# Sorting tokens by expert on the chip, in a two-layer transformer kernel on one core

## What is computed

```python
def _L0_ffn_ref(x, Wg, bg, We, be):
    probs = jax.nn.softmax(x @ Wg + bg, axis=-1)
    idx = jnp.argmax(probs, axis=-1)
    p = jnp.take_along_axis(probs, idx[..., None], axis=-1)[..., 0]
    e_idx = idx % We.shape[0]
    h = jax.nn.relu(jnp.einsum('bsd,edf->besf', x, We) + be[None, :, None, :])
    onehot = jax.nn.one_hot(e_idx, We.shape[0], dtype=x.dtype)
    out = jnp.einsum('besf,bse->bsf', h, onehot) * p[..., None]
    return out
...
    h = _layernorm(x, axis=-1) * (1 + ca) + sa
    x = x + ga * _L0_attn_ref(h, ...)
    h = _layernorm(x, axis=-1) * (1 + cb) + sb
    x = x + gb * _L0_ffn_ref(h, ...)
```

## Time and profile before

| | |
|---|---|
| median of 3 runs | 1774.61 us (1774.03 to 1776.43) |
| the profiled execution's own time | 1779.59 us |
| its span | 1778.3 us |
| TensorE busy | 1671.1 us, 94% of the span |
| VectorE busy | 1507.9 us, 85% |
| ScalarE busy | 1378.1 us, 77% |
| GpSimd busy | 731.7 us, 41% |
| granted TensorE clock | 0.988 of full speed over the span |

### The profile page before, as it was taken

How to read it: one execution, slowest core, us unless ns; L and a number is a source line. 1 busy time by engine, 2 the same in 40 slices (tenths; PEclk the granted TensorE clock), 3 DMA queues, 4 the chain that set the end, 5 groups by cost and what they waited for, 6 DMA issues and landing times.

```text
span 1778.3 us, 54970 instructions
## 1 busy us (share of the span) xinstructions
PE 1671.1 (94%) x23327; PEld 659.4 (37%) x23337; DVE 1507.9 (85%) x2321; ACT 1378.1 (77%) x1934; POOL 731.7 (41%) x1195
## 2 busy tenths in 40 slices
PE   5777999999999999999999999999999999999998
PEld 2542333334333343334333343333433343222224
DVE  4669888898888988899888988899888998999973
ACT  4442678887798778887798877987788877887885
POOL 2321356435544465344654265434654355211110
PEclk9988899999999999999999999999999999999999
DMA  2130111112220322012211222103211122201101
GB/s 71 50 110 24 58 50 58 35 58 55 80 71 14 96 70 72 29 43 74 80 52 34 62 59 87 56 23 91 67 59 36 37 73 71 70 23 50 35 28 34
DMA packets 97233, 99.95 MB, mean 56 GB/s; under 512 B 11116, under 2 KB 81436, under 8 KB 96988
## 3 DMA queue, kind: packets, MB, share of 16 engines
q1 hardware_dynamic: 96188, 95.66, 17.9%
q10 hardware_dynamic: 800, 0.79, 0.1%
HBM read 61.02 MB, written 34.57 MB: 54 GB/s over the span
## 4 chain that ended last, share of the span: by engine, by line
PE 67%; DVE 15%; ACT 13%; issue 3%; DMA 1%; POOL 0%; ACTq 0%; SPq 0%; DVEq 0%
PE pv_psum L818 23%; PE side_psum L551 15%; PE buffer L802 12%; PE buffer L792 10%; DVE row_max L1328 8%; ACT p L1028 7%; PE side_psum L641 2%; PE buffer L551 2%; PE side_psum L608 1%; ACT o_sb L1037 1%; DVE s L1175 1%; ACT s L946 1%; DVE st_f L1087 1%; ACT s L939 1%; ACT hT_b L1017 1%
## 5 line engine op out<-in xcount | busy, mean ns | idle before, releaser
L1328 DVE TENSOR_REDUCE row_max<-buffer 128x2 f32<-128x1024 f32 x1024 | 1234.8, 1219 | 158.7 <-PE buffer L792 145.8
L1028 ACT ACTIVATE p<-buffer 128x1024 f32<-128x1024 f32 x1024 | 1047.5, 1025 | 209.5 <-PE buffer L802 193.6
L818 PE MATMUL pv_psum<-p,v 128*9 128x256 f32 x8192 | 583.9, 381 | 5.8 <-ACT o_sb L1037 5.2
L792 PE MATMUL buffer<-k_ops,q_ops 48*128 48x512 bf16 x2048 | 396.3, 384 | 18.5 <-ACT p L1028 8.8
L802 PE MATMUL buffer<-q_ops,k_ops 51*128 51x512 bf16 x2048 | 400.7, 388 | 6.9 <-DVE row_max L1328 5.8
L818 PEld LDWEIGHTS pv_psum<-p,v 128*9 128x9 f32 x8192 | 149.8, 89 | 316.6 <-issue 233.9
L802 PEld LDWEIGHTS buffer<-q_ops,k_ops 51*128 51x128 bf16 x2048 | 98.2, 93 | 372.0 <-issue 227.7
L1461 POOL TENSOR_TENSOR hm<-masks,hT_f 128x1024 f32<-128x1024 bf16 x56 | 120.3, 2149 | 107.5 <-PE side_psum L551 107.5
L792 PEld LDWEIGHTS buffer<-k_ops,q_ops 48*128 48x128 bf16 x2048 | 99.4, 94 | 117.4 <-ACT p L1028 99.4
L1476 POOL TENSOR_SCALAR nm_parts<-nm 128x16 bf16<-128x16 f32 x64 | 16.2, 253 | 270.4 <-DVE nm L1253 269.9
L551 PE MATMUL side_psum<-we,hm 128*32 128x128 f32 x3648 | 121.0, 274 | 0.0
(11 more groups left out here) (297 smaller groups left out, 1665.1 us busy)
## 6 DMA issues: line engine op xcount, KB each, us to landing
masks<-masks_rows SPq DMA_DIRECT2D x16, 1024.0 KB, 5.8
q_ops<-products SPq DMA_DIRECT2D x128, 96.0 KB
k_ops<-products SPq DMA_DIRECT2D x128, 96.0 KB
products<-q_parts SPq DMA_DIRECT2D x16, 384.0 KB, 2.6
products<-k_parts SPq DMA_DIRECT2D x14, 384.0 KB, 2.8
attention<-o_sb SPq DMA_DIRECT2D x248, 18.0 KB
x<-in_L_attn_inputs SPq DMA_DIRECT2D x8, 512.0 KB, 4.2
products<-q_parts SPq DMA_DIRECT2D x16, 256.0 KB, 3.0
```

The costliest lines, as they stand in the source:

```text
L792: m = e.matmul(buffer[:, hh, :], q_ops[rows_of(hh, K_MAX), slot, of, i * P:(i + 1) * P], k_ops[rows_of(hh, K_MAX), slot, of, halves(half)[ ...
L818: m = e.matmul(pv_psum[q:q + VW, half * QUARTER:(half + 1) * QUARTER], v1[b % 2][:, kb, 2 * hp + hh, :], p_sb[n % KEPT][:, hh, part * QUAR ...
L1028: e.activation(p_sb[n % KEPT][:, :, :], unit("exp", n)[0][:, :, :], ACT.Exp).then_inc(S["exp_done"], 1)
L1328: e.tensor_reduce(mx[pair % 2][:, :, i, half], unit("max", n)[0][:, :, :], axis=AX.X, op=ALU.max).then_inc(S["max_done"], 1)
```

## The change

From batch 1 on, the tokens of a batch are sorted by expert, the experts' products are made on blocks of 64 sorted rows that belong to one expert, and the results are brought back. Batch 0 keeps the masks.

- `ranks`: TensorE counts, for each token, how many before it took the same expert (a product with a triangle of ones and 8 small products with a column of ones), and how many there are of each.
- `places`, `rows`: VectorE and GpSimd make from it each token's row among 24 blocks of 64 (1024 / 64 and 8 that may be partly filled), and each block's expert.
- `scatter`: GpSimd issues 8 indirect transfers, each of 128 rows of the normed tokens, into `rows_in` in HBM; SP's `sorted_load` fetches all 1536 rows in three groups of 4 tiles.
- `experts`: SP reads a block's expert into a register and loads that expert's 64 KB; 24 times, two of them a step, in 12 steps that begin with the scatter.
- `channels_s`, `moe_s`: TensorE transposes a group, then multiplies: each 32 rows with their own block's matrix. The bias comes first, by a one-hot column per block. ScalarE takes the relu, without the gate.
- `sorted_store`: SP stores the result rows; `fetch`: GpSimd issues 8 indirect transfers that gather each token's row; `residual` gets one more pass, the product with the gate.

The buffers of the masks hold the experts' blocks and the transposed groups, those of the masked copies the logits and the third group. The front is laid out 10 steps earlier, the second part of `half_line` now has a place of its own (`HALF_FROM`), after the fetch: `residual` is at steps 62 and 65 of a stretch (before: 26 and 51), `parts` at 73, 74, 78 and 79 (before: 37, 40, 60 and 61). The masked copies are also gone from what `channels` and the last batch's stages wait for.

```diff
+BLOCK = 64
+BLOCKS = N // BLOCK + EXPERTS
+GROUP_TILES = 4
+ROW_GROUPS = BLOCKS * BLOCK // (GROUP_TILES * P)
+
+PIECES, LOADS = 4, 2
...
+def experts_line():
+
+    out = [(2, ("ranks",)), (1, ("places",)), (2, ("rows",))] + [(1, ("scatter", piece)) for piece in range(PIECES)]
+    out += [(3, ("sorted_load",)), (9, ("channels_s", 0)), (1, ("channels_s", 1)), (1, ("moe_s", 0)), (1, ("channels_s", 2)), (0, ("sorted_store", 0)),
+            (1, ("moe_s", 1)), (1, ("sorted_store", 1)), (1, ("moe_s", 2)), (1, ("sorted_store", 2))]
+    return out + [(5 if piece == 0 else 1, ("fetch", piece)) for piece in range(PIECES)]
+def weights_line():
+
+    return [(1, ("experts", piece)) for piece in range(BLOCKS // LOADS)]
...
-FRONT_FROM, WEIGHTS_FROM, BACK_FROM, LOAD_BEFORE = -200, 90, 132, 11
+FRONT_FROM, WEIGHTS_FROM, BACK_FROM, LOAD_BEFORE = -210, 90, 132, 11
+HALF_FROM = (-66, -63)
...
+    for half in range(HALVES):
+        put(half_line(half), 0, HALF_FROM[half])
     put(front_line(), 0, FRONT_FROM)
     for half in range(HALVES):
-        put(half_line(half), 0, at["up", 0, half] + 1)
+        put(choice_line(half), 0, at["up", 0, half] + 1)
+    put(experts_line(), 0, at["onehot", 0, 1])
+    put(weights_line(), 0, at["rows", 0])
...
+        def ranks_stage(b):
...
+            e.matmul(v, above[:, :], oh[:, :, :].rearrange("p t e -> p (t e)"), start=True, stop=False)
+            for t in range(T):
+                m = e.matmul(v[:, (t + 1) * EXPERTS:], one[:, :].broadcast_to([P, P]), oh[:, t:t + 1, :].broadcast_to([P, T - t, EXPERTS]),
+                             start=False, stop=t == T - 1)
...
+        def moe_s(b, g):
...
+            pe.wait_ge(S[f"experts_in{g}"], BLOCKS // ROW_GROUPS * 16 * b)
+            for of_bias in (True, False):
+                for j in range(GROUP_TILES):
+                    for q in range(0, P, COLUMN_TILE):
+                        at = j * P + q
+                        block = (g * GROUP_TILES * P + at) // BLOCK
+                        o = v[q:q + COLUMN_TILE, j * C:(j + 1) * C]
+                        if of_bias:
+                            e.matmul(o, onehot_s[:, block:block + 1].broadcast_to([P, COLUMN_TILE]), be3[:, :], start=j == 0, stop=False)
+                        else:
+                            m = e.matmul(o, hT_s[g % 2][:, at:at + COLUMN_TILE], we_s[:, block, :], start=False, stop=j == GROUP_TILES - 1)
...
+        def scatter(b, piece):
...
+            for t in tiles_of(piece):
+                e.indirect_dma_start(rows_in_dram, bass.IndirectOffsetOnAxis(place[:, t:t + 1], 0), xn_f[:, t, :], None).then_inc(S["scattered"], 16)
+
+        def fetch(b, piece):
+            pool.wait_ge(S["place"], b)
+            pool.wait_ge(S["sorted_out"], ROW_GROUPS * 16 * b)
+            for t in tiles_of(piece):
+                e.indirect_dma_start(xn_f[:, t, :], None, rows_out_dram, bass.IndirectOffsetOnAxis(place[:, t:t + 1], 0)).then_inc(S[f"fetched{2 * t // T}"], 16)
...
-            pool.wait_ge(S["side_act"], side["moe", b, 4 * q + 3].emptied)
+            pool.wait_ge(S[f"fetched{q}"], T // 2 * 16 * b)
+            pool.wait_ge(S[f"gp{q}"], b + 1)
+            after(e.tensor_tensor(xn_f[:, tiles, :], xn_f[:, tiles, :], gp[:, tiles].unsqueeze(2).broadcast_to([P, 4, C]), op=ALU.mult))
...
+        def experts(b, piece):
...
+            for j in range(piece * LOADS, (piece + 1) * LOADS):
+                of = e.value_load(expert[0:1, j:j + 1], min_val=0, max_val=EXPERTS - 1)
+                e.dma_start(we_s[:, j, :], We[bass.ds(of, 1), :, :].rearrange("e c f -> c (e f)")).then_inc(S[f"experts_in{g}"], 16)
```

227 lines of the change are left out of this document (182 added, 45 removed).

## The result

| | before | after |
|---|---|---|
| median | 1775.52 us (1774.03 to 1777.83, 4 runs) | 1851.42 us (1847.61 to 1857.18, 4 runs) |
| the profiled execution's span | 1778.3 us | 1848.5 us |
| granted TensorE clock over the span | 0.988 | 0.976 |

The ratio is 1.0419 with a 95% interval of 1.0401 to 1.0437: **the changed kernel is slower by 76 us**. The sign was forecast; the size, 19 us, was not, though the time lies in the range.

What follows compares the result with a forecast made beforehand. TensorE was taken to bound the kernel. Per batch -9.7 + 7.6 + 4.8 = +2.7 us, seven batches +19: profiled 1779.6 becomes 1798.6, median 1794 us; range 1735 to 1885, the forecast by itself 1779 to 1850.

Steps and rivals of the forecast that it cites:

- sorted instead of masked products: TensorE's products and transposes: 17.2 us per batch gone, 7.5 us new, net 9.7 us less.
- a microsecond of TensorE is a microsecond of the stretch: Rule for a whole stretch (206.0 us, one batch's first exponential to the next): TensorE time saved shortens it equally.
- as long as it stays well above VectorE: Condition on that rule: TensorE's busy time, 199.7 us of a stretch, must stay well above VectorE's 181.3.
- The comparison of two stretches: Evidence for TensorE as bound: the stretch without a next front had 21.4 us less TensorE and was 23.1 us shorter.
- GpSimd's part: Indirect transfers at 1.2 us each and stages moved to steps 62 to 79: waits of together 7.6 us per batch.
- The three waits: VectorE waiting for GpSimd: 2.9 us at step 62, 1.5 by step 68, 3.2 by step 84.
- 13.6 us against 10.7: GpSimd's queue from step 55 against the time until VectorE asks at step 62: a wait of 2.9 us.
- SP's part: 24 expert loads at 1.2 us in steps 23 to 34 delay maxima behind them: TensorE waits 4.8 us per batch.
- The rival of a round trip per register: SP's register read costs 2.03 us per expert, TensorE waits 24.7 us: 1933 us, chance 0.16.
- the exponentials of the pair start at step 48: Deadline for SP's stores of maxima: 73.4 us into the stretch, leaving room of 35.2 us for 40.0.
- The signs to check: If right: TensorE busy near 190 us, some 5 us wait near step 48, three GpSimd waits, stretches of 209 us.
- The last sign: If TensorE's busy time fell by much less than 9.7 us, the sorted products, not the queues, were mis-sized.

Runs made afterwards that it cites:

- plan without sorting: Kernel before, masked copies kept, with the changed kernel's plan (front 10 steps earlier, second part of a half at steps 62 and 65): 1804.11 us, ratio 1.0147.
- constant addresses: Changed kernel with each block's expert matrix loaded from a constant address (block number modulo 8), so SP reads no register: 1795.66 us, ratio 1.0093.
- The pads: Changed kernel with score products made twice in every second step: 1855.68 us for steps 0 to 20, 1861.51 us for steps 88 to 108.
- shortening the queue: Changed kernel with GpSimd's 8 indirect gathers per batch replaced by 2 plain transfers of the first 1024 sorted rows: 1850.52 us, ratio 1.0406.
- the run with the third group late: Third group multiplied at step 53, gathers from step 57: 1856.48 us on the changed kernel, 1836.67 us with experts at constant addresses.

## Why the prediction was wrong in size

The ledger of a stretch, from the windows above, beside the sum of the prediction:

| | forecast | measured | from |
|---|---|---|---|
| sorted instead of masked products | -9.7 | 0.0 (209.82 to 209.80) | plan without sorting against constant addresses |
| GpSimd's queue, and the moved stages | +7.6 | +3.8 (206.05 to 209.82), the moved stages alone | kernel before against plan without sorting |
| SP's queue | +4.8 | +8.1 (209.80 to 217.86) | constant addresses against changed kernel |
| sum | +2.7 | +11.8 | |

The plan without sorting has no indirect transfers, so what these cost, half a microsecond, is within the first row.

- **"a microsecond of TensorE is a microsecond of the stretch"** is the step that failed: its term was -9.7 and measured 0.0. That is the error of the sum, since the other two rows miss by -3.8 and +3.3 and nearly cancel. TensorE's busy time did fall, by 7.0 us in the same plan (199.83 to 192.78). Of the 2.7 that are missing to 9.7, the rank products are 1.0 (9 of 0.17 to 0.19 us, 1.6 instead of 0.6), and the rest has no account; the sorted products were about as priced (3.1 and 1.2 for the bias, summed, for 4.9). But all 7.0 came out of steps 0 to 40, where VectorE is busy 58.5 of 64.1 us even with the copies: that piece gave 2.6, and VectorE then filled 97% of it. Steps 40 to 56, into which six new stages are set, took 2.1 back, with 1.1 more of TensorE's busy time. The rest took 0.5, with 1.1 less of it, for which I have no cause. Over the seven stretches the sorting is worth 3.9 us, 3.2 in the first and 2.4 in the last, less 1.7 in those between; the medians of the two kernels differ by 8. The pads show the same from the other side. I had read VectorE's 181 of 206 us as a mean; the step that I named myself, "as long as it stays well above VectorE", had to be asked of each piece. The comparison of two stretches could not bear the rule either, since VectorE had fallen by 16.3 us there, too.
- **GpSimd's part**: the price of an indirect transfer was right (1.25 us with its gap, against 1.2). The three waits were not there: VectorE waits 2.2 us in two places, against 0.7 in one before, and shortening the queue gave 1 us in the whole run. The count "13.6 us against 10.7" failed in its 10.7: these seven steps take 12.2 us (1.74 a step, not 1.53), VectorE asks 1.6 us after the exponential of step 62 begins, and GpSimd ends 0.03 us before that. That the chain is real is shown by the run with the third group late. What the move of the second half does cost, 3.8 us, comes by another way that no term named. As I read the pieces, it takes TensorE's work out of one that VectorE bounds (2.0 us, and the piece is 0.5 longer) and puts it into one that TensorE bounds (2.8 us, and 3.7 longer). This reading has no run of its own; VectorE also waits 1.3 us more for GpSimd there (2.0 against 0.7), and how the two share the 3.8 is open. That this and SP's part together (11.9) lie near the forecast 12.4 is luck.
- **SP's part**: well sized where it was sized. 1.10 us per expert (forecast 1.20), 30.0 us for the experts with the three sorted loads, a landing of 2.06 (2.0), a wait of 5.3 (4.8) at the place named. Some of this is luck, too: SP was free 41.2 us into the stretch, not 38.2, and step 48 was due at 75.5, not 73.4, two errors that nearly cancel. The rival of a round trip per register fell. Missing was the lower clock after the wait, 2.8 us per batch, more than half of the wait again. Incomplete was also "the exponentials of the pair start at step 48" as the only thing due: the operands of the next pair were due at the same step.
- **The signs to check**: TensorE's busy time per stretch was 195.5, and 192.8 where no half clock stretched it, for 190; the wait near step 48 was as said; the three waits for GpSimd were not; stretches of 217.9, not 209. The last sign would have misled: TensorE's busy time fell by less than 9.7, and yet the sorted products were not what was mis-sized.
- **The range**: the upper end of the forecast by itself, 1850, doesn't follow from its own terms, -9.7 + 9.6 + 10.0 in seven batches, which give 1844. The measured 1851 lies past both.

The Trainium skill (DMA: Bandwidth & Descriptors, Latency and other measured facts) gives about 600 ns as the floor of a register load. The trace does not agree for the instruction: the read of an expert's number takes 0.27 us, and 0.72 pass from its start to that of the transfer (677.75 to 678.47 in the chain), register instructions included. The same section of the Trainium skill gives about 1 us for the software path before its first byte. An indirect transfer takes GpSimd 0.96 us here; when its first byte moves is not seen in the trace.
